# Rounding 256 columns to FP4 on ScalarE and GpSimd, and an f16 band table behind the weights' scales

## The chip, the cores and the metric

The kernel runs on one core of a Trainium2 chip. The metric is the time of one execution on the device, in microseconds. The core has TensorE (PE; its weight loads are PEld), VectorE (DVE), ScalarE (ACT), GpSimd (POOL) and SyncE (SP), which issues the DMAs.

## What is computed

One transformer block with adaptive layer norm, for 32 batches of 512 rows of 256 columns, in f32 (the reference, cut):

```
x = x + ga * attention(layernorm(x) * (1 + ca) + sa)       # 16 heads of 16, softmax over 512
x = x + gb * ffn(layernorm(x) * (1 + cb) + sb)
# attention: scores = q k^T / 4 + 8 * rel_bias[bucket(position difference)]
# ffn: h = silu(fp4(x) @ fp4(w_gate)^T) * (fp4(x) @ fp4(w_up)^T);  out = fp4(h) @ fp4(w_down)^T
# fp4: blocks of 16 columns, scale = max(|x|)/6, x/scale rounded to 0, .5, 1, 1.5, 2, 3, 4, 6, times scale
```

The bias depends only on the difference of positions, which makes it a band: a table of values near the diagonal and two constants beyond. The input of the feed-forward part has 256 columns and is rounded to FP4 once per tile of 128 rows, the hidden values have 704.

## The kernel before

**Order.** Nothing is scheduled by a tool: each engine's program is written out by hand. Time is cut into batches of 16 slots (s = 0 to 15) with four positions each (j = 0 to 3). In every slot TensorE does the scores of four heads against one block of 128 keys (L630, with the band added by the small matmuls of L633), the score products from which VectorE takes row maxima for the next batch (`maxima`, L647), the weighting of the values (`weigh`, L665), and one or two jobs from a table: projections (L704, L711), transposes, and the feed-forward products (L676). The feed-forward part of an earlier tile of 128 rows runs beside the attention; a tile takes four slots, and four tiles are one batch. r = s mod 4 is the slot within the tile. Every engine works its own queue strictly in order and waits on semaphores.

**The maxima.** L647 writes to one of two banks; `reduce_max` on VectorE (L1073, one instruction and its accumulator read) adds the bias and takes the maximum, and frees the bank for the L647 after the next.

**ScalarE.** It takes the exponential of the scores in pairs of heads (L819, at j = 0 and j = 2). TensorE's next scores wait for it. In between stand the copies out of PSUM, such as `ctx_h` (L911), whose low part VectorE then forms (L1118, `low_of`).

**FP4 rounding.** Rounding is done by adding and subtracting a number so large that f32 keeps only the wanted digits. ScalarE squares the scaled value into `magic` (bf16), a constant FLOOR is added, then (value + magic) - magic is the rounded value.
- For the 704 columns (`hidden`, `magic3`): VectorE forms the scales (L1108, L1110, L1112) at r = 3, j = 0; GpSimd divides (L1357) at r = 3; ScalarE squares (L847) at r = 3, j = 3 and adds the constant (L850) at r = 0, j = 0; GpSimd adds, subtracts and multiplies (L1328, L1330, L1332) at r = 0.
- For the 256 columns (`ffn_in`, `magic2`): scales at r = 2, j = 1; GpSimd divides (L1351) at r = 2; ScalarE squares (L842) at r = 2, j = 3; VectorE adds and subtracts with the constant within the operation (L1160, L1162) at r = 3, j = 2; GpSimd multiplies by the scale (L1361) at r = 3, after L1357.

**The band tables.** At the start TensorE makes `band`, 16 heads by 512 values, ScalarE copies it as f32 (L794), SyncE stores it to DRAM (L475) and loads it back with shifted rows: twice 64 partitions x 16 x 256 into `hank1` (L480), and 128 x 16 x 192 into `hank2` (L482). VectorE turns `hank2` into f16 (L1006), `hank1` into f16 (L1008), and for the upper 64 partitions into the rest that f16 leaves (L1009). TensorE spreads the f16 copy of `hank2` with eight matmuls (`spread_band`, L600), VectorE copies each result (L1015) into the table that the maxima use. After it come the scales of the three feed-forward weights (`weight_scales`, L1026 to L1033), then the first `reduce_max`.

## Time and profile before

| | us |
|---|---|
| median of 3 runs (lowest, highest) | 3264.7 (3263.61, 3267.48) |
| the profiled execution, its own time | 3262.75 |
| its span in the trace | 3260.9 |
| busy: PE, PEld | 3137.3, 1876.7 |
| busy: DVE, ACT, POOL | 2765.6, 2088.3, 1732.0 |
| mean granted clock of TensorE | 0.982 of full speed |

Times in the rows are microseconds from the span's start. A row of the timeline gives start, length, engine, line, what is written from what, and in square brackets how long the engine had been idle and what ended that; a row without a bracket started with little or no idle time before it. Matmuls are pipelined, and the length of one includes its way through the array, so that TensorE can show as busy while nothing new enters it.

### The profile page before, as it was taken

The page shows a single profiled execution, that of the slowest core. Times are in us where ns is not written, and L with a number is a line of the kernel's source. Part 1 is how long each engine was busy: PE and PEld are TensorE (multiplying, and loading weights), DVE is VectorE, ACT ScalarE, POOL GpSimd, SP SyncE. Part 2 cuts the span into 40 slices and gives each one's busy share as a digit, 9 for nine tenths or more (in the row PEclk, how much of TensorE's full clock was granted, in tenths as well). Part 3 has the DMA queues.
Part 4 walks back from the last instruction along what each step waited for, and adds up shares of the span by engine and source line. Part 5 has one row for each costly group of instructions (what it writes and reads, how often), then busy time and mean ns, then how long its engine had stood idle before and what let it go on. Part 6 is the DMA issues. An engine that isn't in the chain of part 4 may idle for free.

```text
span 3260.9 us, 67878 instructions
## 1 busy us (share of the span) xinstructions
PE 3137.3 (96%) x22404; PEld 1876.7 (58%) x22404; DVE 2765.6 (85%) x9960; ACT 2088.3 (64%) x3389; POOL 1732.0 (53%) x2104
## 2 busy tenths in 40 slices
PE   4899999999999999999999999999999999999985
PEld 1345566666656566665566665666666565666555
DVE  6678888888888888888888888888888888888865
ACT  2566666666666666666666666666666666666652
POOL 3415555555555555555555555555555555555455
PEclk7899999999999999999999999999999999999997
DMA  8344433334443324444233444332344433244000
GB/s 208 66 79 82 84 75 59 63 70 84 84 87 67 60 59 79 87 84 85 55 66 63 84 87 84 75 59 65 70 84 84 87 66 59 61 79 80 23 22 13
DMA packets 200187, 238.39 MB, mean 73 GB/s; under 512 B 23600, under 2 KB 178640, under 8 KB 199808
## 3 DMA queue, kind: packets, MB, share of 16 engines
q1 hardware_dynamic: 199840, 234.06, 37.1%
q8 instruction: 182, 2.98, 0.4%
q14 instruction: 165, 1.35, 0.2%
HBM read 164.57 MB, written 67.31 MB: 71 GB/s over the span
## 4 chain that ended last, share of the span: by engine, by line
PE 90%; issue 4%; DVE 3%; ACT 2%; DMA 1%; POOL 1%; SPq 0%; POOLq 0%; DVEq 0%; ACTq 0%
PE ps_x L676 25%; PE ps_o L665 15%; PE rings L647 14%; PE rings L630 14%; PE ps_x L704 6%; PE rings L633 5%; PE ps_x L711 3%; PE ps_x L722 2%; PE ps_x L743 2%; PE ps_x L735 1%; PE ps_x L728 1%; PE ps_x L697 1%; ACT probs L819 1%; DMA probs<-band_dram 0%; DVE row_max L1073 0%
## 5 line engine op out<-in xcount | busy, mean ns | idle before, releaser
L1073 DVE CUSTOM_DVE_ANT_0 rings<-rings,band_z 128x512 f32<-128x512 f32 x2048 | 1415.6, 696 | 70.5 <-issue 66.3
L819 ACT ACTIVATE probs<-rings 128x1024 f32<-128x1024 f32 x1024 | 1050.2, 1026 | 587.7 <-PE rings L633 587.5
L647 PE MATMUL rings<-k_rows,q_rows 120*128 120x512 bf16 x2048 | 790.6, 387 | 27.1 <-DVE row_max L1073 25.2
L630 PE MATMUL rings<-q_rows,k_rows 121*128 121x512 bf16 x2048 | 702.3, 383 | 12.3 <-ACT probs L819 11.2
L633 PEld LDWEIGHTS rings<-rev,band_t 128*128 128x128 f16 x5632 | 409.6, 98 | 299.9 <-issue 0.8
L665 PE MATMUL ps_o<-probs,values 128*32 128x512 f32 x4096 | 545.6, 605 | 0.0
L633 PE MATMUL rings<-rev,band_t 128*128 128x64 f16 x5632 | 500.6, 192 | 0.0
L647 PEld LDWEIGHTS rings<-k_rows,q_rows 120*128 120x128 bf16 x2048 | 197.4, 96 | 503.7 <-DVE row_max L1073 371.9
L1357 POOL TENSOR_TENSOR hidden<-hidden,inv 128x704 f32<-128x704 f32 x128 | 178.3, 1393 | 452.2 <-DVE inv L1112 452.2
L676 PE MATMUL ps_x<-w_gu_h,xq_h 128*128 128x512 f32 (+1 forms) x768 | 356.9, 465 | 1.1 <-DVE xq_l L1118 1.1
L1172 DVE SCALAR_TENSOR_TENSOR tanh<-tanh,ps_x 128x256 f32<-128x256 f32 (+1 forms) x384 | 152.3, 397 | 169.6 <-ACT tanh L929 165.3
L1073 DVE DVE_READ_ACCUMULATOR2_ANT row_max<- 128x1 f32 x2048 | 289.1, 141 | 0.0
L676 PE MATMUL ps_x<-w_gu_h,xq_l 128*128 128x512 f32 (+1 forms) x768 | 289.0, 376 | 0.0
L676 PE MATMUL ps_x<-w_gu_l,xq_h 128*128 128x512 f32 (+1 forms) x768 | 285.7, 372 | 0.0
L676 PE MATMUL ps_x<-w_dn_h,hq_h 128*128 128x256 f32 x768 | 240.6, 313 | 18.2 <-DVE hq_l L1126 18.2
L630 PEld LDWEIGHTS rings<-q_rows,k_rows 121*128 121x128 bf16 x2048 | 198.5, 97 | 92.7 <-issue 42.0
L1351 POOL TENSOR_TENSOR ffn_in<-ffn_in,inv 128x256 f32<-128x256 f32 x128 | 79.4, 620 | 303.8 <-DVE inv L1112 303.8
L1328 POOL TENSOR_TENSOR hidden<-hidden,magic 128x704 f32<-128x704 f32 x128 | 200.1, 1563 | 39.4 <-ACT magic L850 38.3
L676 PE MATMUL ps_x<-w_dn_l,hq_h 128*128 128x256 f32 x768 | 219.0, 285 | 0.0
L676 PE MATMUL ps_x<-w_dn_h,hq_l 128*128 128x256 f32 x768 | 218.7, 285 | 0.0
L1287 POOL TENSOR_TENSOR proj<-proj,parts 128x512 f32<-128x512 f32 x128 | 163.7, 1279 | 88.9 <-ACT parts L892 88.9
L1330 POOL TENSOR_TENSOR hidden<-hidden,magic 128x704 f32<-128x704 f32 x128 | 197.5, 1543 | 10.0
(180 smaller groups left out, 6330.4 us busy)
## 6 DMA issues: line engine op xcount, KB each, us to landing
parts_dram<-parts SPq DMA_DIRECT2D x128, 384.0 KB, 2.6
q_rows<-parts_dram SPq DMA_DIRECT2D x384, 128.0 KB, 5.4
k_rows<-parts_dram SPq DMA_DIRECT2D x384, 128.0 KB, 7.9
mod_rows<-mod_rows_dram SPq DMA_DIRECT2D x32, 640.0 KB, 10.0
x_in<-in_x SPq DMA_DIRECT2D x32, 512.0 KB, 5.3
x_mid<-in_x SPq DMA_DIRECT2D x128, 128.0 KB, 2.0
out<-x_mid SPq DMA_DIRECT2D x128, 128.0 KB, 2.2
k_rows<-band_dram SPq DMA_DIRECT2D x2, 1024.0 KB, 9.5
```

Source lines behind the costliest of these rows:

```text
L630: mm(ps_s[:, bank, :], kr[0:ROW_MAX + 1, h, k0:k0 + P], qr[0:ROW_MAX + 1, h, :], start=True, stop=False)
L633: m = mm(ps_s[:, bank, k0 + w * HALF:k0 + (w + 1) * HALF], band_t[:, h, P - w * HALF:2 * P - w * HALF], rev[:, 0, 0:HALF], start=False, st ...
L647: mm(ps_m[:, bank, :], q_rows[par][0:ROW_MAX, h, j * P:(j + 1) * P], k_rows[par][0:ROW_MAX, h, :], start=True, stop=True).then_inc(mscores ...
L665: m = mm(ps_o[32 * j:32 * j + 32, :], values[:, par, kb, h * VW:h * VW + 32], prob(u, j), start=kb == 0, stop=kb == NT - 1)
L676: m = mm(out, left[a][:, dt, :], right[b][:, dt, columns], start=i == 0, stop=i == len(terms) - 1)
L704: m = mm(ps[:, :], w[:, dt, half * P:(half + 1) * P], h_t[:, dt, :], start=dt == 0, stop=dt == DT - 1)
L819: A(prob_pair(s, j), ps_s, ACT.Exp).then_inc(exp_done, 1)
L1073: v.tensor_tensor_reduce(ps, ps, band_z[:, bias:bias + S], 1.0, LOWEST, ALU.add, ALU.max, row_max[:, par, 4 * h + j:4 * h + j + 1]).then_i ...
L1287: q.tensor_tensor(pr, pr, parts[:, p % 2, 0, :], ALU.subtract).then_inc(rest_pool.sem, 1)
L1328: q.tensor_tensor(hid, hid, magic3[:], ALU.add).then_inc(f3_pool.sem, 1)
L1330: q.tensor_tensor(hid, hid, magic3[:], ALU.subtract).then_inc(f3_pool.sem, 1)
L1357: q.tensor_tensor(blocks(hid), blocks(hid), spread(inv3[:], FF // BLK), ALU.mult).then_inc(f2_pool.sem, 1)
```

## The change

It has two parts.

1. The 256 columns are rounded as the 704 are. VectorE's L1160 and L1162 go. ScalarE adds the constant to `magic2` at r = 3, j = 0 (128x256 in bf16). GpSimd adds and subtracts (two operations of 128x256) and multiplies by the scale at r = 3. These three stand in front of the division of the hidden values; before, only the multiplication was there, behind it.
2. The band goes to DRAM as two f16 halves, a high part by ScalarE and the rest by VectorE, both read from PSUM. The tables come back as f16 and in their final place, so that the three conversions on VectorE go. VectorE then does the weights' scales before it copies the eight results of `spread_band`.

```
-            sp.wait_ge(su_act, SA["band"])
-            sp.dma_start(band_dram, band_sb).then_inc(band_stored, 16)
...
+            sp.wait_ge(su_dve, SD["lo"])
+            sp.dma_start(band_dram.bitcast(F16), band_half).then_inc(band_stored, 16)
             sp.wait_ge(su_act, SA["ind"])
...
+            sp.dma_start(hank2_half, bass.AP(vec.tensor, vec.offset,
+                                             [[1, P], [2 * S, H], [1, 3 * HALF]])).then_inc(band_loaded, 16)
             for half in range(2):
+                sp.dma_start(band_t[HALF * half:HALF * (half + 1)],
+                             bass.AP(vec.tensor, vec.offset + S * half,
+                                     [[1, HALF], [2 * S, H], [1, 2 * P]])).then_inc(band_loaded, 16)
...
+                        if (r, j) == (3, 0) and it.has_tile(s, 0):
+                            after(act, f1_act, it.tile(s, 0), "sq")
+                            A(magic2[:], magic2[:], ACT.Identity, bias=floor[:]).then_inc(f1_act.sem, 1)
...
+                step(v.tensor_tensor(band_lo, setup_b[0:H, 0, :], band_hi, ALU.subtract))
+                mark("lo")
...
-                dve.wait_ge(band_loaded, 48)
-                step(v.tensor_copy(hank2_half, hank2))
-                mark("hank")
-                step(v.tensor_copy(band_t[:], hank1))
-                step(v.tensor_tensor(band_t[HALF:P], hank1[HALF:P], band_t[HALF:P], ALU.subtract))
+
+            def band_table():
...
-                if at == (3, 2):
-                    after(dve, f1_act, u, "sq")
-                    v.scalar_tensor_tensor(ffn_in[:], magic2[:], FLOOR, ffn_in[:], ALU.add, ALU.add).then_inc(f1_dve.sem, 1)
-                    after(dve, f1_dve, u, "add")
-                    v.scalar_tensor_tensor(ffn_in[:], magic2[:], FLOOR, ffn_in[:], ALU.add,
-                                           ALU.subtract).then_inc(f1_dve.sem, 1)
...
                     mod_and_bias_tables()
                     weight_scales()
+                    band_table()
...
+                    if r == 3 and it.has_tile(s, 0):
+                        after(pool, f1_act, u, "magic")
+                        q.tensor_tensor(ffn_in[:], ffn_in[:], magic2[:], ALU.add).then_inc(f1_pool.sem, 1)
+                        after(pool, f1_pool, u, "radd")
+                        q.tensor_tensor(ffn_in[:], magic2[:], ffn_in[:], ALU.subtract).then_inc(f1_pool.sem, 1)
+                        after(pool, f1_pool, u, "rsub")
+                        q.tensor_tensor(blocks(ffn_in[:]), blocks(ffn_in[:]), spread(scale2[:], D // BLK),
+                                        ALU.mult).then_inc(f1_pool.sem, 1)
                     if r == 3 and it.has_tile(s, 1):
...
-                    if r == 3 and it.has_tile(s, 0):
-                        after(pool, f1_dve, u, "sub")
-                        q.tensor_tensor(blocks(ffn_in[:]), blocks(ffn_in[:]), spread(scale2[:], D // BLK),
-                                        ALU.mult).then_inc(f1_pool.sem, 1)
```

GpSimd's queue from r = 2 of a tile to r = 0 of the next, in the kernel before (`proj` and `parts` belong to the projections of a later batch):

```order
L1351 TENSOR_TENSOR ffn_in<-ffn_in,inv 128x256
L1294 TENSOR_TENSOR parts<-proj,parts 128x512
L1357 TENSOR_TENSOR hidden<-hidden,inv 128x704
L1361 TENSOR_TENSOR ffn_in<-ffn_in,scale 128x256
L1287 TENSOR_TENSOR proj<-proj,parts 128x512
L1323 TENSOR_TENSOR x_mid<-x_mid,mod_rows 128x256
L1328 TENSOR_TENSOR hidden<-hidden,magic 128x704
```

The same place in the changed kernel, whose lines are numbered a little differently (L1364 is the old L1357):

```order
L1350 TENSOR_TENSOR ffn_in<-ffn_in,inv 128x256
L1293 TENSOR_TENSOR parts<-proj,parts 128x512
L1355 TENSOR_TENSOR ffn_in<-ffn_in,magic 128x256
L1357 TENSOR_TENSOR ffn_in<-magic,ffn_in 128x256
L1359 TENSOR_TENSOR ffn_in<-ffn_in,scale 128x256
L1364 TENSOR_TENSOR hidden<-hidden,inv 128x704
L1286 TENSOR_TENSOR proj<-proj,parts 128x512
L1322 TENSOR_TENSOR x_mid<-x_mid,mod_rows 128x256
```

Three operations on the 256 columns now stand ahead of the division of the hidden values, where one stood behind it.

VectorE's queue at the start in the kernel before, from the end of the modulation tables to the weights' scales (`w_setup` holds the raw weights and the f16 copy of `hank2`, `x_mid` serves as room for the scales):

```order
L1003 COPY context<-mod_rows 32x256
L1006 CAST w_setup<-probs 128x3072
L1008 CAST band_t<-k_rows 128x4096
L1009 TENSOR_TENSOR band_t<-k_rows,band_t 64x4096
L1015 CAST band_z<-rings 128x2x192 x8
L1026 TENSOR_REDUCE x_mid<-w_setup 128x96
L1028 TENSOR_SCALAR x_mid<-x_mid 128x96
L1029 RECIPROCAL x_mid<-x_mid 128x96
```

The same stretch of VectorE's queue in the changed kernel, from the end of the modulation tables to the first row maximum (L1077 is the old L1073):

```order
L1009 COPY context<-mod_rows 32x256
L1030 TENSOR_REDUCE x_mid<-w_setup 128x96
L1032 TENSOR_SCALAR x_mid<-x_mid 128x96
L1033 RECIPROCAL x_mid<-x_mid 128x96
...
L1036 CAST w_o_h<-w_setup 128x512
L1037 TENSOR_TENSOR w_o_l<-w_setup,w_o_h 128x512
L1019 CAST band_z<-rings 128x2x192 x8
L1075 MEMSET wait_pad 128x1
L1077 ISA rings,row_max<-rings,band_z 128x512
```

The three conversions are gone, and the eight copies of the band stand behind the scales.

## Rows read from the trace of the kernel before

**Rows 1.** The page's table of engines: busy us, share of the span, instructions.

```profile
PE 3137.3 (96%) x22404; PEld 1876.7 (58%) x22404; DVE 2765.6 (85%) x9960; ACT 2088.3 (64%) x3389; POOL 1732.0 (53%) x2104
```

**Rows 2.** A stretch: length, busy us (PE, PEld, DVE, ACT, POOL), granted clock, DMA.

```profile
300.00:700.00 400.00, 399.91 (x2919) 242.56 (x2920) 352.31 (x1294) 267.44 (x435) 216.09 (x269) 1.00 0.38 72
```

**Rows 3.** Timeline of the start: VectorE, SyncE's queue (SPq), TensorE.

```profile
34.81 0.28 DVE L1003 COPY context<-mod_rows 32x256 f32<-32x256 f32 x1
...
39.30 1.40 SPq L537 DMA_DIRECT2D parts_dram<-parts  x2
43.78 1.76 DVE L1006 CAST w_setup<-probs 128x3072 f16<-128x3072 f32 x1 [8.69 <-DMA probs<-band_dram]
...
46.49 2.70 SPq L517 DMA_DIRECT2D q_rows<-parts_dram  x6
...
52.36 4.70 DVE L1015 CAST band_z<-rings 128x384 f16<-128x384 f32 x8
...
59.46 0.13 PEld L647 LDWEIGHTS rings<-k_rows,q_rows 120*128 120x128 bf16 x2 [1.00 <-DMA k_rows<-parts_dram]
...
70.54 0.69 DVE L1033 TENSOR_TENSOR w_o_l<-w_setup,w_o_h 128x512 fp32r<-128x512 f32 x1
71.28 0.69 DVE L1073 CUSTOM_DVE_ANT_0 rings<-rings,band_z 128x512 f32<-128x512 f32 x1
```

**Rows 4.** Chain of waits: the band's last load; and the page's DMA issues.

```profile
28.14 15.54 DMA probs<-band_dram
...
parts_dram<-parts SPq DMA_DIRECT2D x128, 384.0 KB, 2.6
```

**Rows 5.** Groups of instructions: busy us, mean ns | idle before, what ended it.

```profile
L842 ACT ACTIVATE magic<-ffn_in 128x256 bf16<-128x256 f32 x128 | 53.7, 419 | 22.4 <-POOL ffn_in L1351 19.8
L838 ACT ACTIVATE ffn_in<-x_mid,shift,rstd 128x256 f32<-128x256 f32 x128 | 76.9, 601 | 116.3 <-POOL shift L1343 113.4 <-PE ps_x L743 2.9
L1361 POOL TENSOR_TENSOR ffn_in<-ffn_in,scale 128x256 f32<-128x256 f32 x128 | 79.5, 621 | 121.4 <-DVE ffn_in L1162 121.4
L1345 POOL TENSOR_TENSOR ffn_in<-ffn_in,mod_rows 128x256 f32<-128x256 f32 x128 | 94.2, 736 | 91.2 <-ACT ffn_in L838 91.2
```

**Rows 6.** Timeline where a batch's slot 15 goes over to slot 0.

```profile
1630.06 1.02 ACT L819 ACTIVATE probs<-rings 128x1024 f32<-128x1024 f32 x1
...
1633.18 1.39 POOL L1357 TENSOR_TENSOR hidden<-hidden,inv 128x704 f32<-128x704 f32 x1 [2.61 <-DVE inv L1112]
...
1634.60 0.79 ACT L847 ACTIVATE magic<-hidden 128x704 bf16<-128x704 f32 x1 [1.68 <-POOL hidden L1357]
...
1635.30 1.01 ACT L819 ACTIVATE probs<-rings 128x1024 f32<-128x1024 f32 x1
...
1637.45 0.42 DVE L1118 TENSOR_TENSOR ctx_l<-ps_x,ctx_h 128x256 fp32r<-128x256 f32 x1 [0.50 <-ACT ctx_h L911]
...
1637.74 1.03 PE L711 MATMUL ps_x<-w_v,h_t 128*128 128x256 f32 x4
...
1637.80 0.70 DVE L1073 CUSTOM_DVE_ANT_0 rings<-rings,band_z 128x512 f32<-128x512 f32 x1
...
1638.61 0.39 PE L647 MATMUL rings<-k_rows,q_rows 120*128 120x512 bf16 x1
```

**Rows 7.** Timeline of GpSimd: L1357 at the batches' ends, first and last.

```profile
289.95 1.39 POOL L1357 TENSOR_TENSOR hidden<-hidden,inv 128x704 f32<-128x704 f32 x1 [2.61 <-DVE inv L1112]
...
2976.24 1.39 POOL L1357 TENSOR_TENSOR hidden<-hidden,inv 128x704 f32<-128x704 f32 x1 [2.61 <-DVE inv L1112]
```

**Rows 8.** Timeline: L1162 in the middle, then L1357 and others near the end.

```profile
1634.88 0.43 DVE L1162 SCALAR_TENSOR_TENSOR ffn_in<-magic,ffn_in 128x256 f32<-128x256 bf16 x1
...
3107.49 1.44 POOL L1357 TENSOR_TENSOR hidden<-hidden,inv 128x704 f32<-128x704 f32 x1 [3.21 <-DVE inv L1112]
...
3107.72 1.49 DVE L1162 SCALAR_TENSOR_TENSOR ffn_in<-magic,ffn_in 128x256 f32<-128x256 bf16 x1
...
3109.96 1.02 ACT L819 ACTIVATE probs<-rings 128x1024 f32<-128x1024 f32 x1 [0.20 <-PE rings L633]
...
3197.01 1.44 POOL L1357 TENSOR_TENSOR hidden<-hidden,inv 128x704 f32<-128x704 f32 x1 [2.80 <-DVE inv L1112]
```

More of the change, by code:

```diff
@@ L353, in build @@
         o_dve = Steps(sem("o_dve"), "recip ctx")
-        f1_act = Steps(sem("f1_act"), "ctxT xh sq")
-        f1_dve = Steps(sem("f1_dve"), "ctxl ga res st ag amax scale inv add sub")
-        f1_pool = Steps(sem("f1_pool"), "xplus eps rstd neg shift mul add xn q")
+        f1_act = Steps(sem("f1_act"), "ctxT xh sq magic")
+        f1_dve = Steps(sem("f1_dve"), "ctxl ga res st ag amax scale inv")
+        f1_pool = Steps(sem("f1_pool"), "xplus eps rstd neg shift mul add xn radd rsub q")
         f2_act = Steps(sem("f2_act"), "xqT tanh0 tanh1 tanh2")
@@ L400, in build @@
         mtmp = context[:].rearrange("p a t d -> p (a t d)")[0:B, 5 * D:8 * D].rearrange("p (a d) -> p a d", a=3)
-        band_sb = o_t[0:H, :]
-        hank1 = flat(k_rows[1]).rearrange("p (h n) -> p h n", h=H)
-        hank2 = wm[:, 0:H * 3 * HALF].rearrange("p (h n) -> p h n", h=H)
+        band_half = o_t[0:H, :].bitcast(F16)
+        band_hi, band_lo = band_half[:, 0:S], band_half[:, S:2 * S]
         hank2_half = w_setup[:, 0:2 * DT * FF].bitcast(F16)[:, 0:H * 3 * HALF].rearrange(
@@ L487, in place_consts @@
             def place_consts():
-                sp.wait_ge(su_dve, SD["end"])
+                sp.wait_ge(su_dve, SD["mrow"])
                 sp.dma_start(q_rows[1][CR], ind[CR].unsqueeze(1).broadcast_to([P - ROWS_QK, H, S])
@@ L593, in _ @@
             pe.wait_ge(qkv_loaded, 80)
+            pe.wait_ge(su_dve, SD["lo"])
             def spread_band():
                 pe.wait_ge(su_act, SA["mod"])
+                pe.wait_ge(band_loaded, 48)
                 for i in range(H // 2):
-                    pe.wait_ge(su_dve, SD["hank"] + (i if i >= 3 else 0))
+                    pe.wait_ge(su_dve, SD["mrow"] + (i - 2 if i >= 3 else 0))
                     mm(setup_a[:, i % 3, 0:6 * HALF], rev[:, 2, :], hank2_half[:, 2 * i:2 * i + 2, :],
@@ L793, in _ @@
             act.wait_ge(su_pe, SP_["rel"])
-            A(band_sb, setup_b[0:H, 0, :], ACT.Copy).then_inc(su_act, 1)
+            A(band_hi, setup_b[0:H, 0, :], ACT.Copy).then_inc(su_act, 1)
             A(c0, setup_b[:, 1, 0:H], ACT.Copy).then_inc(su_act, 1)
@@ L1369 @@
 SA = {"ident": 2, "mod0": 3, "mod": 4, "cols": 5, "band": 6, "rel": 7, "ind": 8}
-SD = {"silu": 2, "scale": 3, "bq": 4, "mrow": 32, "hank": 33, "end": 35 + H // 2}
+SD = {"silu": 2, "scale": 3, "bq": 4, "lo": 5, "mrow": 33, "end": 33 + H // 2}
 SO = {"pads": 2, "end": 3}
```

7 lines of the change are left out of this document (1 added, 6 removed).

## The prediction

> **What bounds the kernel now.** I read the page's table of engines first. TensorE is busy for 3137.3 of 3260.9 us [rows 1]. The table of stretches says where the rest is: from 300 to 700 us TensorE works 399.91 of 400 us at full clock [rows 2]. So in the middle only something that holds TensorE back, or lets it do less, can move the end. The change touches no matmul of the loop. The two ends are different: in the first 130 us and the last 175 us or so TensorE waits on chains through other engines.
>
> The timeline of the start shows one such chain. VectorE finishes its small tables with the COPY at 34.81, then has nothing to do for 8.69 us until the band table has come back from DRAM at 43.78. It converts it, runs the eight CASTs of L1015 (52.36, 4.70 us), only then scales the feed-forward weights, and its last instruction of those is L1033 at 70.54. The first row maximum comes at 71.28 [rows 3], while the projected heads had been ready for TensorE at 59.46 [rows 3]. Everything after is queued behind those maxima.
>
> In the middle, what counts is which waits have no slack. A batch is 16 slots, and the third place of the change, the end of every fourth slot, occurs four times a batch. I followed all four; only the one at the batch's end, where slot 15 goes over to slot 0, is tight [rows 6]. There ScalarE waits 1.68 us for GpSimd's L1357, squares (L847), does the exponential of slot 0 at once after it (1635.30, no idle time in its row), then L850 and L911 back to back. VectorE waits 0.50 us for that L911 before L1118 at 1637.45, the row maximum L1073 follows at 1637.80 and takes 0.70 with the read of its accumulator behind it, and TensorE's L647, whose bank that maximum frees, starts at 1638.61, at once. The four matmuls of L711 ahead of it, issued from 1637.74 on, have streamed out at the same moment. So this chain from L1357 to TensorE has no slack, although TensorE shows no idle time in the row.
>
> **The change, part by part.**
>
> *Start of the kernel: a gain.* Three things leave VectorE's path: L1006, L1008 and L1009, that is everything from 43.78 to 52.36, 8.6 us [rows 3]. The weights' scales move ahead of the eight CASTs and so into the wait for the band. They took from the end of L1015 at 57.06 to 71.23, 14.2 us [rows 3]. New is one subtraction of 16x512 in front, about 0.7 us by L1033, a subtraction with the same 512 elements per partition at 0.69 [rows 3]. New sum for VectorE: tables end at 35.1 + 0.7 = 35.8; scales 14.2, so 50.0 at most (some of those 14.2 us were waits for GpSimd's port, so it may be 46); CASTs 4.7: 50.7 to 54.7. TensorE puts L711 in between as before (52.36+4.70 to 59.46 is 2.4 us), so 53 to 57.
>
> The other condition is the DMA. The band came in three transfers, the last landing 15.54 us after issue [rows 4]; SyncE's store of the projections, issued at 39.30, had landed only at 46.49, when the replication began, and the first L647 could start at 59.46, that is 13.0 us later [rows 3]. With half the bytes the band should be in by 35 to 38, and the store, issued a little after 38, lands in about 3 us as it does elsewhere (2.6 at the median [rows 4]): 41.7 + 13.0 = 54.7. If the transfer is not shortened at all, 59.46 stays. So the first maximum moves from 71.28 to about 56, at best 54, at worst 60. I take 56: **-15.3 us** (-17 to -11). The later steps of the start follow at the maxima's pace; the GpSimd divisions of the weights and the transfers of the second half are due long before their readers. The new waits on SyncE (the store of the band waits for the subtraction, and with it the row indicators and the rows of the modulation) cost nothing: the band store goes first and had waited behind another. TensorE waits for the same subtraction, ahead of transposes that wait longer for ScalarE.
>
> *Slot 3 of each tile: VectorE's two operations go.* L1162 is 0.43 us in the middle [rows 8], L1160 a little more, 1 us together. They stand beside the 18 matmuls of the down projection, at the end of which no row maximum is late, so no L647 waits for them. What I take for this: 0.
>
> *ScalarE's added addition.* Its length is not in the trace. Nearest are L842, a Square of the same 128x256 to the same tile (0.42), and L838, an Identity with two vector operands (0.60) [rows 5]. I take 0.50. It follows the exponential of the slot's first pair (1630.06 + 1.01) and ends at 1631.5 [rows 6]. The next exponential had to wait longer than that for its scores, so the addition is hidden behind TensorE's work and costs ScalarE's queue nothing; without that cover it would cost its 0.5.
>
> *GpSimd's two added operations, and the order.* Each is 128x256 with two full operands: between L1361 (0.62, one operand repeated over blocks) and L1345 (0.74) [rows 5]. I take 0.69. With the multiplication by the scales they now stand **in front of** L1357, before they stood behind it. At the tight place: addition ready 1631.50; two operations of 0.69 and one of 0.62, with 0.05 to 0.08 between them, end at 1633.73. L1357 started at 1633.18 [rows 6]. It is **0.55 us late** (bounds 0.3 with 0.42 and 0.62, 0.75 with 0.60 and 0.74), and by the chain above TensorE is as late, once a batch. At the three other places of a batch L1357 is 0.1 to 0.55 us late too, but there ScalarE sits idle for longer than that, waiting for scores, before the exponential that follows L847. The tight place occurs from 289.95 to 2976.24, every 95.93 us, 29 times [rows 7]: 29 x 0.55 = **+16 us** (+9 to +22).
>
> What the rows show of the port: L1162 takes 0.43 us at 1634.88 with GpSimd idle, and 1.49 at 3107.72, where it ends with the L1357 that ran beside it [rows 8]. The Trainium skill, "SBUF — State Buffer", section on SBUF's two separate sides, calls this an exclusive lock: a VectorE operation in a two-port mode waits for GpSimd's whole instruction. By that rule the small TENSOR_SCALAR ahead of L1112 would now wait for the second of the new operations, and the sum would be some 0.15 us per batch more, 4 us in all; without it the 16 us stand.
>
> *The end.* With the last batch there are no more maxima, and L1112 is ready earlier against the exponentials. At 3107.49 L1357 starts 1.19 us after the exponential of the slot's first pair has ended; the new sequence needs 0.5 + 0.69 + 0.69 + 0.62 + 0.2 = 2.7 us from there, so L1357 is 1.45 late. The exponential at 3109.96 follows L847 with only 0.20 idle and is on the chain [rows 8]: about 1.15 us, in three tiles, this one and its two neighbours. In the tile after them no exponential stands behind it, and all of 1.45 counts. In the four tiles after that, such as the one at 3197.01 [rows 8], where the chain goes L1357, L847, L850, L911, each is 0.55 late, and in the next about 0.4. Sum: 3.45 + 1.45 + 2.2 + 0.4 = **+7.5 us** (+5 to +10).
>
> **Sum.** -15.3 + 16 + 7.5 = +8.2 us. The profiled execution took 3262.75, so 3271; the median of the runs is 2 us above that execution, which gives **3273 us**.
>
> **The rivals.**
>
> *The late L1357 does not reach TensorE in the middle* (faster). For it: that TensorE shows no idle time there, and that my 0.55 is made of durations not in the trace. Against: in all 29 repetitions the rows have the same spacing. The point of decision is the slack of L1357 at the batch's end: if it is over 0.5 us, the 16 us vanish. Then -15.3 + 7.5 = -7.8: 3257. Chance 0.18.
>
> *VectorE's relief lets TensorE run denser* (faster still). VectorE loses 1 us of 24 per tile, and L647 is often put down to it. A quarter of a microsecond per batch back, and no late L1357, would give 3245 to 3252. Against: 399.91 of 400. Chance 0.04.
>
> *The band arrives no sooner.* The number of packets stays and they get shorter. The Trainium skill, "DMA: Bandwidth & Descriptors", Specifications, wants 512 bytes or more for full rate and has smaller ones done by read-modify-write; the rows of 192 columns are now 384 bytes. As a mechanism of this kernel: the transfer takes its 15.5 us [rows 4], replication starts at 46.5, and the first L647 stays at 59.46, a gain of 11.5: 3276. Chance 0.13.
>
> *GpSimd's part is dearer*: 0.74 each plus the port, 0.85 per batch, 24.7 us in the middle and 9 at the end: 3282. Chance 0.12.
>
> The forecast itself has 0.53, with its own spread from 3264 to 3279.
>
> **How the numbers follow.** A measurement tells about 0.2% (6.5 us) from no change: faster is below 3258, slower above 3271. The forecast's spread is cut near its lower middle: about 0.33 of its 0.53 is slower, 0.20 the same; the dear GpSimd and the slow band are slower (0.25, of which I leave 0.02 within); the first rival is half faster and half the same at 3257; the second faster. That gives slower 0.56, same 0.29, faster 0.15 in round numbers. The range leaves out the second rival and the ends: 3256 to 3282.
>
> **What would show it.** In the new profile: the first row maximum at 54 to 60 us instead of 71.28, behind the CASTs and not ahead of them; at the batch's end L1357 starting at once after GpSimd's multiplication by the scales, and the period of a batch 96.3 to 96.6 us instead of 95.93; the exponentials of the last batch's first pairs about 1 us later. I am wrong if the period stays at 95.93 (then slack was there that I did not see), or if the first maximum is early but the first exponential is not.

## The result, and the profile after

| | kernel before | changed kernel |
|---|---|---|
| median of the runs | 3264.34 us (3261.84 to 3267.69, 12 runs) | 3274.07 us (3268.45 to 3276.83, 12 runs) |
| profiled execution, span | 3260.9 us | 3272.2 us |
| TensorE's mean granted clock | 0.982 | 0.983 |

The ratio after to before is 1.0027, with a 95% interval of 1.0018 to 1.0036. The change makes the kernel slower by 9.7 us (0.3%) in the medians, and by 11.3 us between the two profiled executions. Most lines have moved: L1077 is now the row maximum, L820 the exponential, L648 the matmul of the scores that waits for maxima, L851 and L854 the rounding's Square and addition of the 704 columns, L915 the copy of the context, L1122 its low part, L1364 GpSimd's multiplication of the 704 by the reciprocals ("the division" below), L1112, L1114 and L1116 the block scales. L846 is ScalarE's new addition; L1355, L1357 and L1359 are GpSimd's new addition, its subtraction, and the multiplication by the scales.

From the page of the changed kernel, the table of engines and the chain that ended last (shares of the span); the last row is the chain of the kernel before:

```profile
PE 3152.0 (96%) x22404; PEld 1882.3 (58%) x22404; DVE 2660.4 (81%) x9702; ACT 2137.6 (65%) x3517; POOL 1897.5 (58%) x2360
...
PE 72%; issue 9%; ACT 7%; POOL 6%; DVE 5%; DMA 1%; SPq 0%; DVEq 0%; ACTq 0%; POOLq 0%
...
PE 90%; issue 4%; DVE 3%; ACT 2%; DMA 1%; POOL 1%; SPq 0%; POOLq 0%; DVEq 0%; ACTq 0%
```

VectorE has less work, and TensorE has become busier by 14.7 us without one more matmul [rows 1]. Only 72% of the chain lies on TensorE instead of 90%, with 18% instead of 6% on ScalarE, GpSimd and VectorE. The stretch that answers to [rows 2] (length, busy us of PE, PEld, DVE, ACT and POOL, granted clock, DMA):

```profile
300.00:700.00 400.00, 399.17 (x2902) 241.73 (x2900) 338.57 (x1257) 274.66 (x453) 241.69 (x307) 1.00 0.38 72
```

TensorE's idle time there grew from 0.09 to 0.83 us in 400, that is under 0.2 us per batch of the 0.5 that a batch lost (below). The ends of pipelined matmuls are modelled, so short waits between two of them can be counted as busy. This view alone would have missed more than half.

**The start.** Timeline (start, duration, engine, line; in brackets the idle time before and its releaser), answering to [rows 3] and [rows 4]; the second and third rows are from the list of DMA issues, with the KB of each and the time to landing:

```profile
35.83 1.13 DVE L1009 COPY context<-mod_rows 32x256 f32<-32x256 f32 x1
...
band_t<-band_dram SPq DMA_DIRECT2D x2, 512.0 KB, 10.0
w_setup<-band_dram SPq DMA_DIRECT2D x1, 768.0 KB, 8.6
...
38.22 1.23 SPq L536 DMA_DIRECT2D parts_dram<-parts  x2
...
43.22 2.70 SPq L516 DMA_DIRECT2D q_rows<-parts_dram  x6
...
49.94 4.70 DVE L1019 CAST band_z<-rings 128x384 f16<-128x384 f32 x8
...
54.69 2.07 PE L712 MATMUL ps_x<-w_v,h_t 128*128 128x256 f32 x4 [1.27 <-DVE band_z L1019]
...
57.39 1.03 PE L648 MATMUL rings<-k_rows,q_rows 120*128 120x512 bf16 x2 [0.62 <-DMA k_rows<-parts_dram]
...
58.19 0.70 DVE L1077 CUSTOM_DVE_ANT_0 rings<-rings,band_z 128x512 f32<-128x512 f32 x1
```

VectorE no longer waits for the band: tables to 36.96, scales, CASTs to 54.64. The first row maximum starts at 58.19 instead of 71.28, 13.1 us sooner, and the first exponential of the loop moved by the same amount (117.28 instead of 130.36).

**The middle.** Slot 15 going over to slot 0, answering to [rows 6], here with more of GpSimd and VectorE:

```profile
1623.83 1.02 ACT L820 ACTIVATE probs<-rings 128x1024 f32<-128x1024 f32 x1
...
1624.73 0.51 ACT L846 ACTIVATE magic<-magic,pow_consts 128x256 bf16<-128x256 bf16 x1
...
1625.32 0.67 POOL L1355 TENSOR_TENSOR ffn_in<-ffn_in,magic 128x256 f32<-128x256 f32 x1 [0.99 <-ACT magic L846]
1626.06 0.68 POOL L1357 TENSOR_TENSOR ffn_in<-magic,ffn_in 128x256 f32<-128x256 bf16 x1
...
1626.22 0.57 DVE L1114 TENSOR_SCALAR scale<-scale 128x44 f32<-128x44 f32 x1
1626.82 0.43 DVE L1116 RECIPROCAL inv<-scale 128x44 f32<-128x44 f32 x1
...
1626.82 0.62 POOL L1359 TENSOR_TENSOR ffn_in<-ffn_in,scale 128x256 f32<-128x256 f32 x1
1627.40 1.39 POOL L1364 TENSOR_TENSOR hidden<-hidden,inv 128x704 f32<-128x704 f32 x1
...
1628.82 0.79 ACT L851 ACTIVATE magic<-hidden 128x704 bf16<-128x704 f32 x1 [2.13 <-POOL hidden L1364]
...
1631.67 0.42 DVE L1122 TENSOR_TENSOR ctx_l<-ps_x,ctx_h 128x256 fp32r<-128x256 f32 x1 [1.48 <-ACT ctx_h L915]
...
1632.83 0.39 PE L648 MATMUL rings<-k_rows,q_rows 120*128 120x512 bf16 x1 [0.17 <-DVE row_max L1077]
```

Counted from the exponential at the top, the division starts after 3.57 us; before, 3.12 (1630.06 to 1633.18 [rows 6]). It is 0.45 late. The tight chain that the prediction followed is there row by row, and at its end TensorE now waits visibly. What the prediction did not weigh properly is in the two rows at 1626.06 and 1626.22: VectorE's L1114 takes 0.57 us, not the 0.19 of the kernel before, and ends 0.05 us behind the subtraction that runs beside it. The divisions at the first and the last of 29 batch ends, answering to [rows 7]:

```profile
277.34 1.39 POOL L1364 TENSOR_TENSOR hidden<-hidden,inv 128x704 f32<-128x704 f32 x1
...
2977.56 1.39 POOL L1364 TENSOR_TENSOR hidden<-hidden,inv 128x704 f32<-128x704 f32 x1
```

Their distance, 2700.22 us over 28 periods, is a period of 96.44 us instead of 95.94: 0.50 us per batch. This is a mean. Most batches take 96.40 instead of 95.93, that is 0.47 more; the rest of the 0.50 is that every fourth batch of the changed kernel is another 0.16 us longer, which comes to 1.1 us in all. Of the 28 periods, 7 are longer like this in each kernel with the f16 band, and one or none where the band is f32 (the kernel before, runs 2 and 8); why stays open.

Within a batch the place can be read off ScalarE's exponentials. Up to the second pair of slot 15 all 32 keep their distance from the first one within 0.02 us (median over the batches, changed kernel against before); only the step over the batch's end grows. Two such steps, the first from the kernel before, the second from the changed one:

```profile
1727.83 1.03 ACT L819 ACTIVATE probs<-rings 128x1024 f32<-128x1024 f32 x1 [0.82 <-PE rings L633]
...
1731.23 1.01 ACT L819 ACTIVATE probs<-rings 128x1024 f32<-128x1024 f32 x1
...
1625.66 1.03 ACT L820 ACTIVATE probs<-rings 128x1024 f32<-128x1024 f32 x1 [0.43 <-PE rings L634]
...
1629.52 1.01 ACT L820 ACTIVATE probs<-rings 128x1024 f32<-128x1024 f32 x1
```

It was 3.40 us and is 3.86.

**The end.** From 2977.56 on the changed kernel loses another 10.0 us (the division was 1.3 us later than before's there, the span is 11.3 us longer). A division that starts late shows this in its own time before it has cost anything, so divisions and exponentials have to be read together (times of the start in the two traces):

| event | before | changed | later by |
|---|---|---|---|
| exponential behind the last batch end's division | 2978.36 | 2979.68 | 1.32 |
| last exponential ahead of the division at 3087.72 | 3087.33 | 3089.60 | 2.27 |
| that division | 3087.72 | 3091.39 | 3.67 |
| exponential behind it | 3090.16 | 3093.51 | 3.35 |
| exponential behind the next division, the one at 3107.49 | 3109.96 | 3114.36 | 4.40 |
| exponential behind the division after that | 3129.75 | 3136.76 | 7.01 |
| next division, with no exponential behind it | 3147.08 | 3155.48 | 8.40 |
| fifth division after it | 3230.23 | 3240.55 | 10.32 |
| last division | 3242.35 | 3253.90 | 11.55 |
| end of the span | 3260.87 | 3272.19 | 11.33 |

Two parts of this go with TensorE's clock. The three late tiles that have exponentials cost 1.05 to 1.08 us each, but the middle one took 22.4 us from one division to the next where its neighbours took 20.8, and its granted clock is 0.92 instead of 1.00:

```profile
3091.00:3112.00 21.00, 18.69 (x152) 11.11 (x151) 9.81 (x25) 13.52 (x21) 11.96 (x16) 1.00 0.05 14
3112.00:3134.50 22.50, 20.27 (x152) 12.14 (x151) 9.80 (x25) 13.52 (x21) 11.88 (x16) 0.92 0.04 12
```

About 1.6 of the 10 us are this dip. The last step, from 3240.55 to 3253.90, took 1.2 us more than before at a granted clock of 0.73 instead of 0.86, and 0.2 of it came back behind it. Run 2 below has the same rounding and neither: its last step takes 11.96 us (12.12 before), and from its last batch end to its end it takes 291.8 us where the kernel before takes 284.6. So the rounding costs about 7.1 us at the end, and the rest goes with the clock.

### The profile page after: what moved, and what is told of

The parts are those of the page before. It is cut to its first block, busy times and chain, and to the rows that moved or that the text cites. A ratio compares the mean times of both kernels' runs of the same rounds, so it can differ in the third digit from the quotient of the medians.

```text
span 3272.2 us, 68002 instructions
## 1 busy us (share of the span) xinstructions
PE 3152.0 (96%) x22404; PEld 1882.3 (58%) x22404; DVE 2660.4 (81%) x9702; ACT 2137.6 (65%) x3517; POOL 1897.5 (58%) x2360
## 4 chain that ended last, share of the span: by engine, by line
PE 72%; issue 9%; ACT 7%; POOL 6%; DVE 5%; DMA 1%; SPq 0%; DVEq 0%; ACTq 0%; POOLq 0%
PE ps_x L677 21%; PE rings L648 11%; PE ps_o L666 11%; PE rings L631 11%; PE ps_x L705 6%; PE rings L634 4%; PE ps_x L712 2%; ACT probs L820 2%; POOL hidden L1364 2%; PE ps_x L723 1%; PE ps_x L744 1%; ACT tanh L933 1%; DVE row_max L1077 1%; DVE hidden L1176 1%; POOL ffn_in L1357 1%
## 5 line engine op out<-in xcount | busy, mean ns | idle before, releaser
L1077 DVE CUSTOM_DVE_ANT_0 rings<-rings,band_z 128x512 f32<-128x512 f32 x2048 | 1413.4, 696 | 129.8 <-issue 126.0
L820 ACT ACTIVATE probs<-rings 128x1024 f32<-128x1024 f32 x1024 | 1051.1, 1026 | 556.9 <-PE rings L634 556.7
L648 PE MATMUL rings<-k_rows,q_rows 120*128 120x512 bf16 x2048 | 790.8, 387 | 22.2 <-DVE row_max L1077 20.1
L648 PEld LDWEIGHTS rings<-k_rows,q_rows 120*128 120x128 bf16 x2048 | 197.3, 96 | 508.4 <-DVE row_max L1077 371.0
L1077 DVE DVE_READ_ACCUMULATOR2_ANT row_max<- 128x1 f32 x2048 | 288.0, 141 | 0.0
L1355 POOL TENSOR_TENSOR ffn_in<-ffn_in,magic 128x256 f32<-128x256 f32 x128 | 86.3, 674 | 215.4 <-ACT magic L846 215.4
L1286 POOL TENSOR_TENSOR proj<-proj,parts 128x512 f32<-128x512 f32 x128 | 159.3, 1244 | 88.0 <-ACT parts L896 88.0
```

Source lines behind the costliest of these rows:

```text
L648: mm(ps_m[:, bank, :], q_rows[par][0:ROW_MAX, h, j * P:(j + 1) * P], k_rows[par][0:ROW_MAX, h, :], start=True, stop=True).then_inc(mscores ...
L820: A(prob_pair(s, j), ps_s, ACT.Exp).then_inc(exp_done, 1)
L1077: v.tensor_tensor_reduce(ps, ps, band_z[:, bias:bias + S], 1.0, LOWEST, ALU.add, ALU.max, row_max[:, par, 4 * h + j:4 * h + j + 1]).then_i ...
L1286: q.tensor_tensor(pr, pr, parts[:, p % 2, 0, :], ALU.subtract).then_inc(rest_pool.sem, 1)
```

## Experiments

Every kernel here is one or two moves away from the kernel before or from the changed one. Medians stand beside the kernel before as timed in the same series (3264.6, then 3262.96, then 3266.68 us, for runs 1 to 4, 5 to 8 and 9 to 11; the series ran on three different chips, so medians of different series are compared by their ratios to before). "Period" is the distance of the divisions at the first and last batch end over 28, as above; "late" is the start of the division after the exponential of slot 15's first pair, less the 3.12 us of before (read to 0.01 us).

| kernel | median, us | ratio to before (95%) | period, us | late, us |
|---|---|---|---|---|
| before | | | 95.94 | 0 |
| changed | 3274.07 | 1.0027 (1.0018 to 1.0036) | 96.44 | 0.45 |
| 1 band only | 3253.59 | 0.9963 (0.9951 to 0.9976) | 95.99 | 0 |
| 2 rounding only | 3284.81 | 1.0060 (1.0047 to 1.0073) | 96.40 | 0.45 |
| 3 multiplication behind | 3266.69 | 1.0005 (0.9996 to 1.0014) | 96.36 | 0.39 |
| 4 the same in slot 15 only | 3270.29 | 1.0017 (1.0008 to 1.0026) | 96.36 | 0.38 |
| 5 subtraction and multiplication behind | 3251.89 | 0.9964 (0.9950 to 0.9978) | 95.96 | 0.01 |
| 6 all three behind | 3259.51 | 0.9987 (0.9978 to 0.9996) | 96.09 | 0 |
| 7 f16 band, old order | 3273.32 | 1.0031 (1.0020 to 1.0043) | 96.42 | 0.45 |
| 8 new order, f32 band | 3254.33 | 0.9973 (0.9963 to 0.9983) | 95.94 | 0 |
| 9 subtraction between | 3273.77 | 1.0021 (1.0013 to 1.0030) | 96.62 | 0.62 |
| 10 run 5 again | 3253.84 | 0.9960 (0.9947 to 0.9974) | 95.99 | 0 |
| 11 run 1 again | 3253.18 | 0.9959 (0.9947 to 0.9972) | 96.00 | 0 |

### 1 and 2: the two halves of the change apart

Run 1 is the kernel before with every hunk of the diff on the band and on the order, and none on the rounding; run 2 the other way round.

> Only the second half of the change on the kernel before: the f16 bias band with the weights' scales in front of its table; the FP4 rounding of the 256 columns stays on VectorE. My theory (the start gives 13.1 us, the middle and the end lose 24 us, and all of that loss is the rounding's): first L648 near 57.4 us, first row maximum near 58.2, the division by GpSimd's multiplication back at its place of before in every batch (period 95.93 us), span 3260.9 - 13.1 = 3247.8, median near 3251. Rival A, that part of the loss comes with the earlier start (the end of the kernel is set by something that does not move with the start): 3254 or more, with the shift of the last divisions shrinking towards the end. Rival B, that the start's gain does not go through: 3264.

> Only the first half on the kernel before: the rounding of the 256 columns by ScalarE (one addition) and GpSimd (addition, subtraction, multiplication ahead of the division of the 704); the band stays f32. My theory: first row maximum at 71.3 as before, the division in slot 15 later by 0.50 us more in each batch (period 96.44), +14 in the middle and +10 at the end: 3264 + 24 = 3288. Rival, that the loss needs the second half too (or that the two parts overlap): under 3280.

Measured: -11.0 us for the band and +20.2 for the rounding, beside forecasts of -13 and +24. Their sum, +9.2, is the changed kernel's +9.7: within the noise the halves don't add to or take from one another. Run 2 stays under its forecast mostly because that counted the dip of the clock at the end as the rounding's. In run 1 the period is 95.99 and 90% of the chain lies on TensorE, as before; in run 2 the first exponential is where it was (130.57 beside 130.36 us) and the period is 96.40. So the rounding carries all of the loss.

### 3 and 4: the multiplication behind the division

```diff
                     low(it, s)
                     ... radd, rsub: GpSimd's addition and subtraction
-                        q.tensor_tensor(blocks(ffn_in[:]), ..., spread(scale2[:], D // BLK), ALU.mult)
                     if r == 3 and it.has_tile(s, 1):
                         ... the division of the 704
+                    if r == 3 and it.has_tile(s, 0):
+                        q.tensor_tensor(blocks(ffn_in[:]), ..., spread(scale2[:], D // BLK), ALU.mult)
```

Run 4 does this for slot 15 alone.

> The changed kernel with one operation of GpSimd put back: in all slots the multiplication by the 256 columns' scales runs behind the division of the 704, the new addition and subtraction stay in front. Theory (late division at slot 15 sets the middle's pace): the division starts at about 1626.75 instead of 1627.40 in the timeline's slot, 0.65 earlier, and the period falls from 96.44 back to 95.9, 14 us less in the middle; the end keeps part of its loss; 3274 - 14 - 2 to 5 = 3255 to 3258. Rival A, ScalarE's added 0.50 us of work in each batch sets the pace: nothing changes, 3274. Rival B, VectorE's operation held up beside GpSimd's multiplication (L1114, 0.57 instead of 0.19) sets it: the hold-up moves to another place, 3270 to 3274.

> As the kernel with the multiplication behind the division, but only in slot 15, the one place where the trace of before showed TensorE's wait for ScalarE's queue behind the division; in the other three slots the order is the changed kernel's. Theory: the whole gain of the middle comes from this one slot, period 95.9, 3274 - 14 = 3260, with at most 3 us between it and the kernel that does it in all slots. Rival, the loss is GpSimd's load in every slot: a quarter of the gain, 3270.

My theory fell: of the middle's 14 us only 2 came back (period 96.36), in either kernel. The timeline of run 3 shows why:

```profile
1617.91 1.01 ACT L820 ACTIVATE probs<-rings 128x1024 f32<-128x1024 f32 x1
...
1620.15 0.68 POOL L1357 TENSOR_TENSOR ffn_in<-magic,ffn_in 128x256 f32<-128x256 bf16 x1
...
1620.31 0.57 DVE L1114 TENSOR_SCALAR scale<-scale 128x44 f32<-128x44 f32 x1
1620.91 0.43 DVE L1116 RECIPROCAL inv<-scale 128x44 f32<-128x44 f32 x1
...
1621.42 1.39 POOL L1361 TENSOR_TENSOR hidden<-hidden,inv 128x704 f32<-128x704 f32 x1 [0.58 <-DVE inv L1116]
```

GpSimd is free 0.58 us before it can start the division, which now waits for the reciprocals: they are late themselves, because L1114 was held up by the subtraction. In the changed kernel two causes lie one over the other, GpSimd's queue (0.45) and the held-up VectorE operation (0.38). Taking one away uncovers the other. What the two runs do agree on is the place: moving the multiplication in all four slots gives the middle no more than moving it in slot 15. What else lies between the two kernels is mostly the end, where the other slots count too: from the last batch end on run 3 takes 289.9 us and run 4 292.6.

### 5 and 6: remove both causes

Run 5 puts subtraction and multiplication behind the division, and leaves the addition in front, which ends before L1114 starts. Run 6 puts the addition behind as well.

```diff
                         q.tensor_tensor(ffn_in[:], ffn_in[:], magic2[:], ALU.add)
-                        q.tensor_tensor(ffn_in[:], magic2[:], ffn_in[:], ALU.subtract)
-                        ... the multiplication by the scales
                         ... the division of the 704
+                        q.tensor_tensor(ffn_in[:], magic2[:], ffn_in[:], ALU.subtract)
+                        ... the multiplication by the scales
```

> The changed kernel with two of GpSimd's operations behind the division of the 704 in all slots: the subtraction and the multiplication; the addition stays in front and ends before VectorE's L1114. New theory after the two runs with only the multiplication moved (period 96.37 instead of 96.44, where 95.93 was forecast): in those the subtraction still ran beside VectorE's L1114, which took 0.57 instead of 0.19 us, so that the reciprocals, and with them the division, stayed 0.39 late. Two causes lay one over the other, 0.45 by GpSimd's queue and 0.38 by the hold-up, and both have to go. Expected: L1114 back to 0.19, the gaps of 0.14 and 0.26 to 0.33 us on TensorE gone, period 95.9 to 96.0, and a median 11 to 13 us under that of the multiplication-only kernel (3266.7): 3254 to 3256. Rival A, ScalarE's addition (0.51 us in each tile, which all these kernels keep) sets the pace: period stays 96.37, 3266. Rival B, the rounding of the 256 is now late for TensorE's transposes (the chain behind the division is 2.2 us): L1114 back to 0.19 but a new gap before the transposes L736, 3258 to 3262.

> As the one before, but GpSimd's addition runs behind the division too. Theory: L1114 at 0.19 and the division on time as there; GpSimd's chain behind the division is 0.7 us longer and ends about 6.5 us after the start of the exponential L820, the transposes L736 start 6.8 after it, so the middle stays at 95.9 to 96.1; the end, where the addition now lies on the chain, costs up to 2 us more: 3254 to 3259. Rival: the transposes wait 0.1 to 0.5 us in each tile that has them, up to +14: 3268.

Run 5, the same place:

```profile
1616.14 1.02 ACT L820 ACTIVATE probs<-rings 128x1024 f32<-128x1024 f32 x1
...
1617.63 0.67 POOL L1355 TENSOR_TENSOR ffn_in<-ffn_in,magic 128x256 f32<-128x256 f32 x1 [0.98 <-ACT magic L846]
...
1618.54 0.19 DVE L1114 TENSOR_SCALAR scale<-scale 128x44 f32<-128x44 f32 x1
1618.76 0.43 DVE L1116 RECIPROCAL inv<-scale 128x44 f32<-128x44 f32 x1
...
1619.27 1.39 POOL L1359 TENSOR_TENSOR hidden<-hidden,inv 128x704 f32<-128x704 f32 x1 [0.96 <-DVE inv L1116]
PE 90%; issue 4%; DVE 3%; ACT 2%; POOL 1%; DMA 1%; SPq 0%; POOLq 0%; DVEq 0%; ACTq 0%
```

L1114 takes 0.19, the division starts after 3.13 us, the period is 95.96 and the chain lies on TensorE to 90%. The median is 11.1 us under the kernel before, while the changed kernel's is 9.7 above its own. ScalarE's addition is still in it, so that was not a cost. The groups of L1114's 44-column form, from 300 to 2976 us, tell the same over the whole middle (count, busy us, mean ns, idle time before; changed kernel, then run 5). The mean of 355 ns is over the four slots of a batch: in the changed kernel the medians are 0.57 us in slot 15 and 0.43, 0.23 and 0.19 in the others.

```profile
L1114 DVE TENSOR_SCALAR scale<-scale 128x44 f32<-128x44 f32 x110 | 39.0, 355 | 3.8
```

```profile
L1114 DVE TENSOR_SCALAR scale<-scale 128x44 f32<-128x44 f32 x111 | 20.6, 186 | 3.8
```

Run 6 overshoots: the median is 7.6 us above run 5, half a microsecond over what I had expected. In its middle, TensorE's transposes of the rounded columns (L736) start 0.12 us later behind slot 15 than in run 5, and each batch is 0.13 us longer (period 96.09); from the last batch end on it takes 290.9 us, where run 5 takes 287.2. So the moved work has a best place between the two chains, the division's and the transposes'.

### 7 and 8: f16 or order?

Run 7 is the changed kernel with the band's table again ahead of the weights' scales; run 8 is the kernel before with this alone:

```diff
                     mod_and_bias_tables()
-                    weight_scales()
                     band_table()
+                    weight_scales()
```

(shown for run 7; in run 8 `band_table()` is cut out of `mod_and_bias_tables()`, with the three conversions of the f32 band, and called behind `weight_scales()`.)

> The changed kernel, but the table of the band is built ahead of the weights' scales, as before. VectorE has no conversions of the band any more (8.5 us: 1.77, 2.31, 4.43), but it waits for the band's load as before, which ends about 37 (f16, issued from about 23); the rows L1019 (4.70) and then the scales (12.9) follow from 37.4 to 55. Theory that the order is worth nothing once the band is f16, since the load has ended when VectorE comes to it and the sum of VectorE's work is the same: first row maximum 57 to 58.5, 3274. Rival, that the order is part of the gain: TensorE's band matmuls and V projections start later or the replication's issue is delayed, first maximum at 60 to 66, 3277 to 3282.

> The kernel before with the order alone: the weights' scales ahead of the band's conversions and table, which stays f32; FP4 rounding as before. In before VectorE waits for the band's load from 35.9 to 43.8 (7.9 us); with the scales (12.9 us) in that gap the load is hidden, and VectorE goes on with conversions (8.5) and table (4.7): 36.9 + 12.9 + 8.5 + 4.7 = 63.0, and V projections of 2.1 behind it, so first maximum near 65.7 instead of 71.3. Theory (the start's gain of 13 is 5.5 of order and 7.5 of f16): 3264 - 5.5 = 3259. Rival, that without the f16 load the order gains nothing (the replication waits for something else): 3264.

Run 7 is the changed kernel's time (3273.32, first maximum at 58.02). Run 8 gains 8.6 us, more than the 5.5 expected:

```profile
46.87 1.76 DVE L1009 CAST w_setup<-probs 128x3072 f16<-128x3072 f32 x1
...
51.00 5.25 DVE L1012 TENSOR_TENSOR band_t<-k_rows,band_t 64x4096 f16<-64x4096 f32 x1
...
56.28 4.70 DVE L1018 CAST band_z<-rings 128x384 f16<-128x384 f32 x8
...
63.75 0.70 DVE L1076 CUSTOM_DVE_ANT_0 rings<-rings,band_z 128x512 f32<-128x512 f32 x1
```

The conversions start at 46.87, not at 49.8: the tables ended 0.8 us sooner than in the changed kernel, and the scales took 10.8 us rather than 12.9 in that place. The first maximum comes at 63.75, 7.5 sooner. The two parts of the band's edit are not two gains: each ends VectorE's wait for the band's load, the order by filling it (8.6 us of the 11.0 of run 1), f16 by shortening it and sparing the conversions (by itself as much as both together). With f16 in, the order is worth nothing that can be measured.

### 9: late by the queue alone

This is run 5's kernel, but in slot 15 GpSimd waits for the reciprocals, runs the subtraction, then the division, so that nothing lies beside L1114:

```diff
                         after(pool, f2_dve, it.tile(s, 1), "inv")
+                        if g == 3 and it.has_tile(s, 0):
+                            q.tensor_tensor(ffn_in[:], magic2[:], ffn_in[:], ALU.subtract)
                         ... the division of the 704
```

> As the kernel with subtraction and multiplication behind the division, but in slot 15 alone the subtraction goes between: GpSimd first waits for VectorE's reciprocals (L1116) and then runs the subtraction (0.67) ahead of the division, so it can't lie beside L1114. This makes the division late by GpSimd's queue alone. Theory, by which TensorE follows the division one to one (0.45 late gave 0.497 us in each batch, 0.38 late gave 0.423): L1114 stays at 0.19, the division starts 0.70 to 0.75 late, period 95.95 + 0.7 = 96.65 to 96.7, 0.7 x 29 = 20 us: 3252 + 20 = 3272. Rival, by which the middle's loss came through the row maximum held up behind L1114 and the late division alone is mostly covered: under 3260.

```profile
1626.86 1.02 ACT L820 ACTIVATE probs<-rings 128x1024 f32<-128x1024 f32 x1
...
1629.24 0.19 DVE L1114 TENSOR_SCALAR scale<-scale 128x44 f32<-128x44 f32 x1
...
1629.97 0.68 POOL L1361 TENSOR_TENSOR ffn_in<-magic,ffn_in 128x256 f32<-128x256 bf16 x1 [0.95 <-DVE inv L1116]
...
1630.60 1.39 POOL L1362 TENSOR_TENSOR hidden<-hidden,inv 128x704 f32<-128x704 f32 x1
...
1636.03 0.39 PE L648 MATMUL rings<-k_rows,q_rows 120*128 120x512 bf16 x1 [0.38 <-DVE row_max L1077]
```

3273.77 is 19.9 us above run 5's kernel as timed in the same series (run 10), where 20 were expected. L1114 is at its 0.19 and the division 0.62 late, and the period grew by 0.68. With the kernels above this is a scale of doses: 0.01 late gives 0.02 us per batch, 0.39 gives 0.42, 0.45 gives 0.50, 0.62 gives 0.68. Every one of these four has the f16 band and its longer fourth batches; by the median batch the same doses give 0.00, 0.39, 0.47 and 0.65. TensorE follows the division at the batch's end one to one, whatever makes it late.

### 10 and 11: is VectorE's relief worth anything?

Runs 5 and 1 once more, side by side; the only difference is who rounds the 256 columns.

> The kernel with subtraction and multiplication behind the division once more, beside the next one on the same chip. 3251 to 3254.

> The second half of the change alone once more, for the comparison with the run before it: does taking the rounding's 0.98 us in each tile from VectorE give anything when nothing is late? Theory that VectorE is not the bound: both the same within 2 us, 3252 to 3255. Rival, that VectorE's relief makes TensorE denser once the division is on time: this one 4 us or more slower.

3253.84 (3252.03 to 3254.03) and 3253.18 us (3249.06 to 3255.47), five runs each: the same within 2 us. Both beat the kernel before, by 0.4% (ratios 0.9960 and 0.9959). About 1 us of work per tile taken from VectorE brings nothing that can be measured, even where nothing is late.

## Why the prediction was right, and where it wasn't

The forecast was 3273 us for the median, from a sum of 8.2 us above the profiled execution of before; 3274.07 was measured. The mechanism was right in its main lines; that the total came within 1 us in the medians is in part luck, since the profiles missed it by 3 and the terms erred both ways:

| step | forecast | measured |
|---|---|---|
| start | -15.3 | -13.1 |
| middle | +16 | +13.9 from the first to the last batch end, 14.4 for 29 |
| end | +7.5 | +10.0, of it about 2.6 with the clock (dip 1.6, last step 1.0); 7.1 in run 2, which has neither |
| sum | +8.2 | +11.3 (medians: +9.7) |

- **Start.** The mechanism was right: VectorE's gap is filled, the conversions are gone, and the first maximum is near 56 (58.19; 54 to 60 were given). Mis-sized is the DMA term: the store of the projections, issued at 38.22, took 5.0 us until the replication at 43.22, where I took "about 3 us" from a median over the whole kernel, and the first L648 came 14.2 us after that, at 57.39, not 13.0. VectorE's side was nearly as late: CASTs to 54.64, then L712's 2.07, so that L648 could start at 56.76 at the earliest in any case. The rival of a band that arrives no sooner is out: its loads took 8.6 and 10.0 us to landing, not 15.54 [rows 4], and VectorE never waited for them. (The rule on short rows that the text names beside that rival decides nothing here: with half the bytes the loads landed sooner. What short rows cost by themselves no run isolates.)
- **Who gets the start's gain.** The text spoke of both parts of the edit as if each were needed. Runs 7 and 8 show that they overlap.
- **VectorE's two operations: 0.** Right, by runs 10 and 11.
- **ScalarE's addition: 0.50, hidden.** It takes 0.51, and run 5 holds it without loss.
- **GpSimd's operations ahead of the division: 0.55 late.** They take 0.67 and 0.68 (0.69 taken), the division is 0.45 late, and each batch loses 0.50. The place, that it is the only one in a batch, and that TensorE has no slack there: right, by runs 4, 5 and 9 and by the exponentials, which lose time nowhere else.
- **The cause behind that term was half told.** The working put everything on GpSimd's queue. By it, run 3 had to win back the 14 us, and it won back 2. The row of L1162 [rows 8] had shown VectorE's operation held until GpSimd's had ended (it ended 0.28 us behind it, not with it as the text has it), and the prediction named the small TENSOR_SCALAR as the next to be held, but priced this as 0.15 us on top. It is 0.38, and not on top: it makes the reciprocals late below the queue's own lateness. The rule of the Trainium skill, "SBUF — State Buffer", section on the two separate sides of SBUF, by which whichever of the two engines starts first keeps the shared ports for its whole instruction and the other waits, agrees with the trace: 0.57 us beside the subtraction, which had started 0.16 us earlier, and 0.19 without. So the number was near with one cause too few. A forecast of the whole change can't tell two overlapping causes from one; a forecast of a partial undo can.
- **End.** The terms held up one by one. The three tiles with exponentials lost 1.05 to 1.08 us each without the dip, where 1.15 was forecast; in the tile after them the division is 1.40 late and all of it counts, where 1.45 was forecast; the next four lost 1.54 together, not 2.2, and the next 0.38, as against 0.4. That is 6.5 of the forecast 7.5. Without a term in the sum were 0.95 us in the four tiles ahead of them, where the late division reached the exponentials too (0.37, 0.22 and 0.37 us in three of them), and the 2.6 us that go with the clock.
- **Two totals of the rivals** are a microsecond too low: by the text's own terms, a band that arrives no sooner gives 3264.7 - 11.5 + 16 + 7.5 = 3277, and the dearer GpSimd 3264.7 - 15.3 + 24.7 + 9 = 3283.

The rival by which the late division doesn't reach TensorE is refuted by the doses, that of a denser TensorE by runs 10 and 11, and that of a dearer GpSimd by its operations (0.67 and 0.68 us, not 0.74) and by the 0.50 us per batch, where it had 0.85.

## What to carry to other kernels

When an operation is moved to another engine, ask what it stands in front of there, and put it behind whatever feeds the chain without slack: with the same three operations in another order, the whole change went from 10 us lost to 11 won. The 11 are the band's, though; the moved rounding brought nothing in any order, because VectorE was not what TensorE waited for. Ask also what runs beside the new place on an engine that the moved operation can hold up, because the hold-up can fall on the very operation that the queue waits for. And when a partial undo wins back much less than the sum says, look for a second cause under the first before giving up the place: here lateness by the queue and lateness by the held-up operation lay one over the other, and only removing both showed either.

## What the runs showed of the hardware

- **Which of VectorE's operations GpSimd holds up.** The TENSOR_SCALAR of L1114, which reads and writes SBUF (the on-chip buffer), is held: 0.57 us instead of 0.19. The REDUCE, the RECIPROCAL and the row maximum that stood beside GpSimd's work in the same slot took their usual time (0.88, 0.43, 0.69). The COPY of L1009 at the start took 1.13 us beside GpSimd's L1286, where the same COPY (L1003) took 0.28 [rows 3]. The subtraction of the f32 band in run 8 took 5.25 us instead of 4.42 before, at another place beside GpSimd, which fits, but wasn't isolated.
- **VectorE holds up GpSimd as well.** At the start of the kernel before, two of GpSimd's operations start 0.02 us behind VectorE's L1009 (47.90 to 52.32) and take 6.53 us together; the same two in the changed kernel, which has no such subtraction, take 2.31:

```profile
47.92 6.53 POOL L1287 TENSOR_TENSOR proj<-proj,parts 128x512 f32<-128x512 f32 x2 [9.51 <-ACT parts L892]
...
44.65 2.31 POOL L1286 TENSOR_TENSOR proj<-proj,parts 128x512 f32<-128x512 f32 x2 [5.56 <-ACT parts L896]
```

- **The prologue's length goes with the granted clock.** The changed kernel and run 3 have the same instructions before the loop. The first maximum came at 58.19 and 57.33, the first exponential of the loop at 117.28 and 112.45 us. Between the two, the granted clock differs, 0.70 in the changed kernel and 0.78 in run 3:

```profile
58.19:117.28 59.09, 43.68 (x101) 15.50 (x101) 39.75 (x177) 21.02 (x29) 16.06 (x15) 0.70 0.68 112
57.33:112.45 55.12, 39.08 (x101) 13.97 (x101) 39.55 (x177) 20.90 (x29) 16.35 (x16) 0.78 0.70 116
```

  Runs 4 and 6, again with the same instructions there, took 60.02 us at 0.70 and 56.34 at 0.77. That is up to 5 us between single profiles that no edit made, so a start's gain is read from the medians or from the first maximum, not from one span. Why the clock differs stays open.
- **A long tile at the end.** In several profiles (runs 1, 3, 4 and 5 among them) one of the last tiles is 1.4 to 1.7 us longer than its neighbours, another one each time. In run 5 it was the 12 matmuls here, which took 4.07 us where the same 12 of the neighbouring tiles took 2.32:

```profile
3188.19 4.07 PE ps_x L677 x12
```

  The granted clock was 0.54 over these 4.07 us and 0.99 and 1.00 over the two neighbours' 2.32. In this part of every kernel, the one before included, the granted clock goes to and fro between its two levels (0.80 of full speed from 3170 to 3240 us before). Why the lower one falls on a given tile's matmuls stays open.
